# A two-block conv/attention/scan kernel: the batch loop written out, its side work placed, the scans cut in halves, and sixteen matmuls of zeros at the start

## The reference, cut to what matters

```
x = x + L0(groupnorm(x))     # linear attention: q, k, v, o = W x; elu+1; softmax weights of k;
                             # rope; kv = k_rope^T v; res = (q_rope kv) * z;
                             # lepe = 5x5 depthwise conv of v; out = Wproj ((res + lepe) * o)
x = x + L1(groupnorm(x))     # layernorm; 4 groups of 32 channels through one mamba; skip; layernorm; proj

# the mamba, for each of 4*8 sequences of 256 steps, d = 64 channels, s = 16 states
xt, z = split(xc @ W_in.T);  u = silu(conv4(xt) + b);  dt, B, C = split(u @ W_x.T)
delta = softplus(dt @ W_dt.T + b_dt);  A = -exp(A_log)
h_t = exp(delta_t * A) * h_{t-1} + (delta_t * u_t) * B_t
y_t = sum_s h_t * C_t + u_t * D;  out = (y * silu(z)) @ W_out.T
```

## Time and profile before

| | |
|---|---|
| median of 3 runs | 365.04 us (363.38 to 365.83) |
| span of the profiled execution | 364.0 us |
| VectorE busy | 272.0 us, 75% |
| TensorE busy | 273.2 us, 75% |
| ScalarE busy | 218.2 us, 60% |
| GpSimd busy | 201.7 us, 55% |
| mean granted TensorE clock | 0.861 |

### The profile page before, as it was taken

How to read it: one execution, slowest core, us unless ns; L and a number is a source line. 1 busy time by engine, 2 the same in 40 slices (tenths; PEclk the granted TensorE clock), 3 DMA queues, 4 the chain that set the end, 5 groups by cost and what they waited for, 6 DMA issues and landing times.

```text
span 364.0 us, 5551 instructions
## 1 busy us (share of the span) xinstructions
PE 273.2 (75%) x1882; PEld 130.7 (36%) x1882; DVE 272.0 (75%) x334; ACT 218.2 (60%) x408; POOL 201.7 (55%) x135
## 2 busy tenths in 40 slices
PE   1596894899594866987998669878966776965763
PEld 1264552344232333533453235325522211421321
DVE  1632156999212599787999897979999988999992
ACT  2334777563843798359775985697667637552211
POOL 0030302576250279827875797377758666876760
PEclk9999898569788799898799999988999756585598
DMA  7230409730159907782689177908881792197000
GB/s 254 97 90 14 104 16 339 287 88 24 45 127 273 354 34 192 248 306 80 161 292 333 38 206 251 338 27 236 252 307 43 255 309 102 54 331 251 0 14 14
DMA packets 27075, 61.73 MB, mean 170 GB/s; under 512 B 2992, under 2 KB 14896, under 8 KB 27056
## 3 DMA queue, kind: packets, MB, share of 16 engines
q1 hardware_dynamic: 26768, 60.88, 52.6%
q10 hardware_dynamic: 288, 0.61, 0.5%
HBM read 54.62 MB, written 6.86 MB: 169 GB/s over the span
## 4 chain that ended last, share of the span: by engine, by line
PE 30%; DVE 20%; DMA 16%; POOL 9%; issue 9%; ACT 9%; SPq 6%; POOLq 0%; DVEq 0%; ACTq 0%
DVE hst L1190 7%; PE F L430 6%; POOL hst L958 6%; DMA V<-v_scratch 6%; PE DB L554 3%; DVE DB L1165 3%; DMA bc_scratch<-bc 3%; PE Y L581 3%; DVE hst L1177 3%; DVE DB L1161 3%; DMA Cs<-bc_scratch 2%; SPq L253 2%; PE F L408 2%; DVE hst L1180 2%; SPq L229 2%
## 5 line engine op out<-in xcount | busy, mean ns | idle before, releaser
L958 POOL TENSOR_TENSOR hst<-hst,Cs 128x1024 f32<-128x1024 f32 x48 | 113.3, 2361 | 87.9 <-DVE hst L1190 87.9
L1190 DVE TENSOR_TENSOR_SCAN hst<-dec,DB 128x1024 f32<-128x1024 f32 x48 | 109.6, 2283 | 4.4 <-ACT dec L841 3.4
L841 ACT ACTIVATE dec<-dlt,negA 128x1020 f32<-128x1020 f32 x60 | 67.6, 1142 | 17.8 <-DVE hst L1180 9.8
L1165 DVE TENSOR_TENSOR DB<-DB,Bs 128x1024 f32<-128x1024 f32 x48 | 59.0, 1228 | 10.9 <-PE DB L554 5.7
L581 PE MATMUL Y<-hst,CCs 128*32 128x256 f32 x512 | 52.0, 453 | 10.8 <-POOL hst L955 7.0
L955 POOL TENSOR_TENSOR hst<-hst,Cs 128x512 f32<-128x512 f32 x31 | 38.7, 1269 | 15.8 <-DVE hst L1177 15.7
L430 PE MATMUL F<-V,wpatch 128*32 128x256 f32 x512 | 34.8, 395 | 5.0 <-DMA V<-v_scratch 5.0
L581 PEld LDWEIGHTS Y<-hst,CCs 128*32 128x32 f32 x512 | 15.0, 120 | 48.1 <-issue 25.7
L554 PE MATMUL DB<-du,CCs 32*128 32x512 f32 x64 | 24.7, 855 | 4.7 <-DVE DB L1161 4.0
L909 POOL TENSOR_TENSOR tq<-QK,W0s 128x512 f32<-128x512 f32 x8 | 9.0, 1124 | 34.4 <-DVE QK L1071 34.4
L430 PEld LDWEIGHTS F<-V,wpatch 128*32 128x32 f32 x512 | 14.8, 110 | 20.5 <-DMA V<-v_scratch 6.7
(11 more groups left out here) (175 smaller groups left out, 507.9 us busy)
## 6 DMA issues: line engine op xcount, KB each, us to landing
Bs<-bc_scratch SPq DMA_DIRECT2D x32, 512.0 KB, 6.0
Cs<-bc_scratch SPq DMA_DIRECT2D x32, 512.0 KB, 6.9
dlt<-delta_scratch SPq DMA_DIRECT2D x15, 512.0 KB, 5.9
V<-v_scratch SPq DMA_DIRECT2D x32, 200.0 KB, 3.9
XN<-xn_scratch SPq DMA_DIRECT2D x28, 128.0 KB, 3.4
delta_scratch<-delta SPq DMA_DIRECT2D x16, 128.0 KB, 4.2
v_scratch<-vpad SPq DMA_DIRECT2D x8, 211.5 KB, 2.1
bc_scratch<-bc SPq DMA_DIRECT2D x8, 128.0 KB
```

The source lines that it names most:

```text
L841: af(dec[g % 4][:, :, 1:T], dlt[2 * j + g // SG][:, :, 1:T], ACT.Exp, scale=negA[:, g:g + 1]).then_inc(S("decay_ready"), 1)
L958: tt(hst[g % 4][:], hst[g % 4][:], Cs[g % SG][:], ALU.mult).then_inc(S("hc_ready"), 1)
L1165: v.tensor_tensor(flat(BIN), flat(DU), Bs[g % SG][:], ALU.mult).then_inc(S("b_ready"), 1)
L1190: v.tensor_tensor_scan(hst[g % 4][:], flat(dec[g % 4][:]), flat(BIN), 0.0, ALU.mult, ALU.add).then_inc(S("h_ready"), 1)
```

## The change

Five things change together.

1. **No loop.** `periods` becomes `program`: all 64 units are written out on every engine, and every step of every chain of all 8 batches has a number of its own in a table (`places`). No block of steps stands between batch 0 and batch 1 any more; the steps of batches 1 to 3 that stood there are among the units of batch 0 or before unit 0. The 64 loads of `Bs` and `Cs` are placed one by one, and a load of `Bs` waits for `b_ready` alone, not for GpSimd's `hc_ready`.
2. **Half scans everywhere, skewed.** On VectorE every unit is four pieces of 512: bin half 0 of unit u, scan half 1 of unit u-1, scan half 0 of unit u, bin half 1 of unit u. The broadcast of `du` signals each half (`feed`). GpSimd multiplies whole units up to batch 5 as before.
3. **Batch 0's beginning.** v is projected first, into `F1`, o into `BIN`; so the q-k softmax doesn't wait for v and o. `Bs` of unit 0 comes from two matmuls with a new 0/1 table `pickb` and two ScalarE copies, not from the DRAM scratch. Batch 0's gate `zs` is copied raw, and its silu is done later beside batch 1's.
4. **A third `zs` buffer**, so that a gate can be made earlier.
5. **Sixteen matmuls of zeros**, 128x256 into `Y`, 10 before and 6 after the first group averages, on a tile `warm` that VectorE clears first. Nobody reads them.

```
-        def periods(eng, chains, places, start, unit, finish):
...
-            run(works, START + SEGMENTS, 7 * SEGMENTS)
-            with eng.Fori(0, (B - 4) // 2) as pair:
-                period(2 * pair + 1, 1)
-                period(2 * pair + 2, 0)
...
+        def program(chains, places, unit, finish):
+
+            works = [begin(chain, b, steps) for chain in chains for b, steps in places[chain.__name__].items()]
+            segment(works, START - 1)
+            for b in range(B):
                 for g in range(GROUPS):
...
+                    seg = iter(range(START + SIDES * (GROUPS * b + g), START + SIDES * (GROUPS * b + g + 1)))
+                    unit(b, b % 2, g, lambda: segment(works, next(seg)))
...
             def setup():
+                pe.wait_ge(S("warm_zero"), 1)
+                spin(10)
                 pe.wait_ge(S("group_loaded"), 16)
                 averages(0, 0, 1, F0)
+                spin(6)
...
+            def spin(n):
+
+                for _ in range(n):
+                    mm(Y[:, 0:T], warm[:, 0:P], warm[:], start=True, stop=True)
...
+                if b == 0:
+                    yield
+                    pe.wait_ge(S("xg0_ready"), b + 1)
+                    project(F1[:, T:2 * T], 2).then_inc(S("v_done"), 1)
...
+                for half in range(2):
+                    rows = slice(2 * DS * half, 2 * DS * half + 2 * DS)
+                    last = mm(BIN[:, half, :], wt("pickb")[rows], bc[rows, :], start=True, stop=True)
+                last.then_inc(S("b0_done"), 1)
...
+            def feed(b, j):
+
+                for kg in range(2):
+                    for half in range(2):
+                        yield
+                        pe.wait_ge(S("du_ready"), b + 1)
+                        wait(pe, ("b_half", "b_ready")[half], GROUPS * b + SG * kg)
...
+            def scan_half(u, half):
+
+                dve.wait_ge(S(("b_half", "b_ready")[half]), u + 1)
+                dve.wait_ge(S("decay_ready"), u + 1)
+                wait(dve, "y_summed", u - 3)
...
+            def unit(b, j, g, side):
+                u = GROUPS * b + g
+                bin_half(b, g, 0)
                 side()
...
+                if u > 0:
+                    scan_half(u - 1, 1)
                 side()
...
+                scan_half(u, 0)
                 side()
+                bin_half(b, g, 1)
                 side()
...
+                "lepe": {
+                    0: (3, 4.5, 6, 6.5,),
```

More of the change, by code:

```diff
@@ L126, in halved @@
         def halved(b):
-            return isinstance(b, int) and b >= B - HALVED
+            return b >= B - HALVED
         def halves(tile, half):
@@ L134, in advance, with begin @@
         def advance(work):
[L136 to L141, removed]
+            next(work[0], None)
+            work[1] = next(work[2], IDLE)
+        def begin(chain, b, places):
+            work = [chain(b, b % 2), 0, iter(places)]
             advance(work)
@@ L254, in spill, with loads @@
                         S("delta_out"), 16)
[L256 to L265, removed]
+            def loads(b, j):
+                for k in range(SG):
+                    for which, (copies, sem) in enumerate(((Bs[k], "b_copied"), (Cs[k], "c_copied"))):
+                        if (b, k, which) == (0, 0, 0):
+                            continue
+                        yield
+                        sp.wait_ge(S("bc_out"), 16 * (b + 1))
+                        if b > 0:
+                            sp.wait_ge(S(("b_ready", "hc_ready")[which]), GROUPS * (b - 1) + SG + k + 1)
+                        rows = bc_dram[j, which, SG * k:SG * k + SG]
+                        sp.dma_start(copies[:], rows.unsqueeze(0).broadcast_to([DD, SG, 4 * T])).then_inc(
+                            S(f"{sem}_{k}"), 16)
             def load_delta(b, j, kg):
-                if kg == 0:
-                    sp.wait_ge(S("delta_out"), 16 * 2 * (b + 1))
+                sp.wait_ge(S("delta_out"), 16 * 2 * (b + 1))
+                wait(sp, "decay_ready", GROUPS * (b - 2) + SG * (kg + 1))
                 rows = delta_dram[j, DD * kg:DD * kg + DD].rearrange("d h n -> d (h n)")
@@ L315, in weights @@
-            def weights(b, j):
-                yield from ()
-            places = {
-                "tail": {
-                    1: (102.938, 110.562, 123,),
+            def unit(b, j, g, side):
+                for _ in range(SIDES):
+                    side()
+            places = {
+                "front": {
+                    0: (0, 0.5,),
+                    1: (1, 1.5,),
+                    2: (3.5, 5,),
+                    3: (9, 9.5,),
+                    4: (16.5, 18.5,),
+                    5: (25, 25.5,),
+                    6: (33, 34.5,),
+                    7: (42, 43,),
@@ L335, in _ @@
                 },
             }
-            periods(sp, (weights, front, lepe, mid, tail, back, lead), places, lambda: None, unit, lambda: None)
+            program((front, mid, tail, lead, loads, back), places, unit, lambda: None)
             sp.wait_ge(S("stored"), 16 * B)
@@ L546, in back, with unit @@
                 done.then_inc(S("proj2_done"), 1)
-            def broadcast_du(b, j, kg):
-                pe.wait_ge(S("du_ready"), b + 1)
-                wait(pe, "b_ready", GROUPS * b + SG * kg)
-                for half in range(2):
-                    p0 = DI * half + DD * kg
-                    last = mm(DU[:, half, :], wt("pick")[p0:p0 + DD], du[j][p0:p0 + DD, :], start=True, stop=True)
-                last.then_inc(S("du_bc"), 1)
-            def collect(b, j, g):
+            def unit(b, j, g, side):
+                side()
+                side()
                 u = GROUPS * b + g
-                pe.wait_ge(S("hc_ready"), u + 1 if not halved(b) else u)
-                if isinstance(b, int) and b == 0 and g == 0:
+                if not halved(b):
+                    pe.wait_ge(S("hc_ready"), u + 1)
+                if u == 0:
                     pe.wait_ge(S("decay_ready"), SG)
@@ L637, in _ @@
                 },
             }
-            periods(pe, (weights, front, lepe, mid, tail, back, lead), places, start, unit, finish)
+            program((weights, front, lepe, mid, tail, lead, feed, back), places, unit, lambda: None)
         @block.scalar
```

775 lines of the change are left out of this document (419 added, 356 removed), and 39 rows, old and new, of the table places.

## The result

The changed kernel takes **353.5 us** (median of 4 runs, 349.8 to 354.8) where before takes 365.4 beside it: a ratio of 0.970, 95% interval 0.961 to 0.979. It is faster, by 12 us where I forecast 32, and 3.5 us outside my range. The profiled execution took 354.8 us, its span is 353.0. Some executions of a kernel ran over 1.5% above its fastest, at a lower granted clock; all medians and ratios from here on are of the others.

The account below looks back on a forecast made before the run. Bound: VectorE's stream of bins and scans, and what keeps it waiting. Terms 56.4 + 76.1 + 99.0 + 99.8 = 331.3 us of span, plus 1.0 to the median and 0.7 for a stall, gave 333 us; range 321 to 350.

Parts of the forecast that it names:

- Batches 2 to 4: 106.4 to 99.0: Three middle batches: 33.0 us each instead of 35.5, 7.4 us won.
- floor of 31.4: Least time of a batch on VectorE: eight units at 3.42 us plus 4.0 us of side steps.
- leg 2: Batch 1's chain, from `XN` through DRAM to `xp`: stays 8.1 us.
- leg 4: Batch 1's chain, `bc` to first bin: grows from 10.0 to 14.5 us, batch 2's `XN` write being ahead in SP's queue.
- Batch 1 at 33.0: Batch 1's units: no hole and a usual batch of 33.0 us, where they took 43.5.
- batches 5 to 7: 101.2 to 99.8: Last three batches and the end: only batch 5 gains, 1.4 us from halving; the final chain stays 10 us.
- Batch 0 and the hole: 43.1: From batch 0's first bin at 56.4 to batch 1's at 99.5: 43.1 us, where it was 54.9.
- The four legs: Batch 1's chain from `u3` to its first bin: 11.5, 8.1, 10.5 and 14.5 us, together 44.6.
- The stall before unit 4: Batch 0: VectorE stands from about 71 to 77 us, waiting for a broadcast of `du`; costs nothing.
- Beginning: 56.4: Start to batch 0's first bin: 56.4 us instead of 57.95, the chain's gain nearly spent on side work.
- 3.42 a unit: VectorE's time per unit with skewed half scans: 3.42 us, against 3.59 for whole ones.
- The first rival: Batches stay at 35.5 us, TensorE being the next bound; batches 1 to 4 cost 10 more: 343 us, chance 0.22.

Follow-up runs that it names:

- in the second: The changed kernel measured and traced once more, with nothing changed: 350.0 us, ratio 0.963 to the kernel before.

## Why the prediction was wrong, step by step

- **Batches 2 to 4: 106.4 to 99.0** is the step that failed: 109.2 in this trace and 105.5 in the second, so the three together won little or nothing. The 33.0 a batch is what VectorE's work allows: 33.2 in batch 2, and 99.5 for all three without the trips. (My floor of 31.4 was a little low: VectorE was busy 32.0 to 32.2 a batch, as before.) But I took the 1.5 us of idle from the halved batches at the end, where no later batch's chain runs beside them, so none of their TensorE steps waits for shifted copies. I allowed 1.5 us of idle a batch, and the first trace has 12.7 in these three. The sum lacked a term for the trips, which hold VectorE in two ways. On TensorE, `XN` to `xp` took 12.4 us against the 8.1 of leg 2, ahead of collects and broadcasts. On SyncE, the loads of `Bs` stand behind the trips, and bins waited for them. From batch 1 to 4 TensorE cost 9.6 us of waits and `Bs` 6.6 in the first trace; the split is not shown by a run. I saw the first stall in batch 0 and SyncE's order in leg 4, and didn't ask where else they stand.
- **Batch 1 at 33.0** (36.5) and part of **batches 5 to 7: 101.2 to 99.8** (105.9) fail in the same way: batch 1 took 33.9 without trips, and its losses in the first trace are the two waits for `Bs` of 2.14 and 1.81 us, the first of them the stall at the second bin for which I had put 0.7. "The tiles that the first units need are issued first" did not hold: the four copies stand before the second `Bs`. In the last term bins waited 4.8 us for `Bs`. But 103.3 of it were left without trips. 1.1 of that is the half scan of batch 4 that the skew puts behind batch 5's first bin, which I had not counted, and the 1.4 for halving batch 5 never came: VectorE was busy 91.7 us there, 90.7 before. The rest was not tried.
- **Batch 0 and the hole: 43.1** measured 42.8, and the hole closed. The four legs held one by one: from batch 1's `u3` at 57.2 they took 10.6, 8.9, 11.9 and 12.8 us, where I had 11.5, 8.1, 10.5 and 14.5. The stall before unit 4 came too, 5.5 us.
- **Beginning: 56.4** measured 58.7 (57.9 again). Zeros until 7.5 was nearly right (the averages start at 7.91). What they give back was over-sized: 2.2 us, not 2.5 against 2 lost, since 3.0 were lost.
- **3.42 a unit** held. VectorE's timeline after, two pairs of half scans in a row:

```profile
312.54 2.32 DVE L1251 TENSOR_TENSOR_SCAN hst<-dec,DB 128x512 f32<-128x512 f32 x2
314.78 1.27 DVE L1243 TENSOR_TENSOR DB<-DB,Bs 128x512 f32<-128x512 f32 x2
315.96 2.32 DVE L1251 TENSOR_TENSOR_SCAN hst<-dec,DB 128x512 f32<-128x512 f32 x2
```

  They stand 3.42 us apart. But halves as such don't win 1.4 a batch: in the old order they cost 1.6% of the kernel (writing out the loop alone: 0.4%, not told from nothing).
- **The first rival** had the right engine and nearly the right size (10 us on batches 1 to 4, measured 13.7) and the wrong reason, TensorE's work; it is TensorE's order and the loads of `Bs`. That its size came near was luck.

## What to carry to other kernels

When a hole closes, every transfer that the hole had covered is due earlier: go through each wait on a DMA on the in-order engines and ask what stands behind it, batch by batch, not only at the place of the change. The engine that issues the DMAs is one of them: a write that waits for its data holds every load behind it. Take the idle time of a steady stage from a stage that has the same side chains. Leaving a transfer out, beside leaving out as many bytes elsewhere, helps to tell lateness from bandwidth in two runs, if both stand at the same place in the queue. Where a wait is labelled "issue", look for the semaphore that rose just before its end.

## What the runs showed of the hardware that was not expected

- Copies of 128 KB issued from ScalarE's queue landed in a median of 7.2 us, from SP's in 3.9, with the same 512 KB loads on SyncE's queue, though at another place in the batch.
- Ten matmuls of zeros at the very start ended at about 8 us (twenty instructions in 6.88), and at 1.46 us for three projections the fast price held, but it was lost again by L408 after waits of 2.2 and 2.4 us, while PEclk for 16 to 20 us showed 0.51.
- The same wait at `xp` lasted 5.37 and 2.42 us in two profiled runs of one kernel.
- Four copies of 200 KB issued within 1.5 us of each other (`V4`, from 231.39 us) landed after 3.5, 4.1, 4.4 and 7.8 us; without XN4's trip the same four took 3.4, 4.0, 4.4 and 7.8. The last one alone set the wait of 3.40 us at `lepe`.
